# An LSTM step on one core: gate products of 512 columns cut into 256, and a verdict given by the sequencer

## What is computed

```python
def step(carry, x_t):
    h, c = carry
    sel_in = jnp.concatenate([h, c, x_t], axis=-1)
    logits = sel_in @ W_sel.T + b_sel
    onehot = jax.nn.one_hot(jnp.argmax(logits, axis=-1), Sx, dtype=x_t.dtype)
    g_all = jnp.einsum('bi,sgi->bsg', x_t, W_ih) + jnp.einsum('bh,sgh->bsg', h, W_hh) + b_ih + b_hh
    g = jnp.einsum('bsg,bs->bg', g_all, onehot)
    h2, c2 = _lstm_activate(g, c)        # sigmoid(f)*c + sigmoid(i)*tanh(g); sigmoid(o)*tanh(c)
    return ((h2, c2), h2)
```

## Time and profile before

| | |
|---|---|
| runs | 7712.02 us median of 3 (7709.5 to 7713.49) |
| the profiled execution | 7713.46 us, span 7711.7 us |
| PE busy | 6634.8 us (86%), 85,214 matmuls |
| PEld busy | 3513.4 us (46%) |
| DVE busy | 3545.5 us (46%) |
| ACT, POOL busy | 1004.7 us (13%), 945.3 us (12%) |
| granted TensorE clock, mean | 0.963 |

### The profile page before, as it was taken

One profiled execution on the slowest core, in us unless ns is written; L12 is line 12 of the kernel. 1 busy time (PEld: TensorE's weight loads), 2 busy tenths in 40 slices (PEclk: granted clock), 3 DMA queues, 4 the chain that ended last, 5 costly groups with the idle time before them and its releaser, 6 DMA issues. The chain is left out here.

```text
span 7711.7 us, 250693 instructions
## 1 busy us (share of the span) xinstructions
PE 6634.8 (86%) x85214; PEld 3513.4 (46%) x85215; DVE 3545.5 (46%) x16895; ACT 1004.7 (13%) x4031; POOL 945.3 (12%) x2829
## 2 busy tenths in 40 slices
PE   3467998899999998888888888888888888888888
PEld 3433444655555554444444444444444444444444
DVE  5523112355555554444444444444444444444444
ACT  0011001311111111111111111111111111111111
POOL 5703112200000000000000000000000000000000
PEclk6588998999999999999999999999999999999999
DMA  3220001622222210000000000000000000000000
GB/s 83 0 68 0 0 0 40 224 78 81 80 84 77 83 56 8 4 8 4 8 8 4 8 4 8 6 7 8 4 8 7 6 8 4 8 4 8 8 4 24
DMA packets 292938, 220.00 MB, mean 29 GB/s; under 512 B 137196, under 2 KB 268652, under 8 KB 290609
## 3 DMA queue, kind: packets, MB, share of 16 engines
q1 hardware_dynamic: 162612, 160.58, 6.2%
q10 hardware_dynamic: 106110, 59.01, 3.0%
q0 software_dynamic: 24192, 0.10, 1.0%
HBM read 160.28 MB, written 59.36 MB: 28 GB/s over the span
## 5 line engine op out<-in xcount | busy, mean ns | idle before, releaser
L1021 PE MATMUL ps<-WH,hparts 128*17 128x512 f16 x49760 | 2969.1, 380 | 148.9 <-DVE hparts L864 63.7
L1021 PEld LDWEIGHTS ps<-WH,hparts 128*17 128x17 f16 x49760 | 1305.0, 91 | 1316.2 <-DVE hparts L864 242.7
L840 DVE STREAM_TRANSPOSE gateT<-ps 128x512 f32<-128x512 f32 x1250 | 896.0, 717 | 2097.2 <-PE ps L1057 2088.0
L1091 PE MATMUL ps<-WH 128*128 128x512 f16 x4970 | 1246.1, 381 | 0.0
L467 POOL COPY xT<-hfull 128x4 f32 x1250 | 239.9, 192 | 5386.9 <-DVE hparts L862 5386.9
L1008 PE MATMUL ps<-wselT,acts 128*1 128x4 f32 x10000 | 430.5, 166 | 407.1 <-DVE acts L852 407.1
L972 PE MATMUL ps<-O,Adj 128*128 128x512 f16 x3000 | 650.3, 380 | 77.2 <-DVEq L749 77.2
L1091 PEld LDWEIGHTS ps<-WH 128*128 128x128 f16 x4970 | 404.6, 97 | 630.8 <-issue 278.7
L581 ACT ACTIVATE gateT<-gblk 128x16 f32 x1250 | 289.3, 231 | 2660.9 <-DVE pick L835 2618.4
L585 ACT ACTIVATE acts<-gates 128x16 f32<-128x16 f32 x1250 | 269.8, 216 | 2239.8 <-DVE gates L844 2239.8
L1065 PE MATMUL ps<-xT,wih_next 128*128 x2048 | 501.1, 388 | 65.1 <-DMA wih_next<-in_w_ih 34.0
(11 more groups left out here) (141 smaller groups left out, 4547.4 us busy)
## 6 DMA issues: line engine op xcount, KB each, us to landing
wih_next<-in_w_ih SPq DMA_DIRECT2D x256, 256.0 KB, 2.9
gblk<-gate_inputs ACTq DMA_DIRECT2D x48, 800.0 KB, 5.0
gate_inputs<-gx_next SPq DMA_DIRECT2D x64, 500.0 KB, 2.6
wst<-in_w_hh ACTq DMA_DIRECT2D x32, 512.0 KB, 7.6
wih<-in_w_ih SPq DMA_DIRECT2D x16, 1024.0 KB, 8.6
adjacency<-Adj SPq DMA_DIRECT2D x2, 6400.5 KB, 24.7
Adj<-adjacency SPq DMA_DIRECT2D x2, 6400.0 KB, 26.8
gate_inputs<-gstage SPq DMA_DIRECT2D x16, 500.0 KB, 6.0
```

What stands on the lines that cost most here:

```text
L840: dve.transpose(gateT[:, :, 0:32], gate_ps.rearrange("p (c q) -> p c q", q=32)).then_inc(turned, 1)
L1021: nc.tensor.matmul(gate_ps[32 * j:32 * j + 17, :], hparts[:, k, :], WH[:, s * KC + k, part, j, :], start=(k == 0 and part == 0), stop=(k = ...
L1091: nc.tensor.matmul(ps[:, 2, :], WH[:, 0, 0, 0, 0:P], WH[:, 0, 0, 0, :], start=True, stop=True)
```

## The change

The 32 matmuls of 512 columns become 64 of 256 columns, over the same weights. `hparts` gets two columns more; the first 4 matmuls of each eight read it from column 1 and take the first two gates, the other 4 read it from column 0 and take the other two gates, so that these land one row lower (rows 1 and 17 beside 0 and 16) in the same 256 columns of PSUM. The transpose reads 256 columns in place of 512. The seal is gone: the last four products count `guess_mm`, and DVE also waits for `settled`, which either the sequencer counts, where guess and verdict agree, or the last four of the repeated products. The branches on the guess stand ahead of the logits, so that each of the four copies now holds logits, products and verdict; the guess for the next step is read behind the products. On DVE, c comes before `osig`, and `owsel` is made from `acts` directly; all logits wait for `owsel_ready`.

```diff
-        gateT = sb("gateT", [P, G * SUB, 33], f32)
+        gateT = sb("gateT", [P, 2 * SUB, 48], f32)
...
-        hparts = sb("hparts", [P, SUB, 17], f16)
+        hparts = sb("hparts", [P, SUB, 19], f16)
...
-                dve.wait_ge(gates_mm, n)
+                dve.wait_ge(guess_mm, n4)
+                dve.wait_ge(settled, n4)
                 dve.transpose(gateT[:, :, 0:32], gate_ps.rearrange("p (c q) -> p c q", q=32)).then_inc(turned, 1)
...
-                pe.wait_ge(c_ready, n)
+                pe.wait_ge(owsel_ready, n)
                 for k in range(SUB):
                     nc.tensor.matmul(logit_ps, acts[:, G * SUB + k:G * SUB + k + 1], wselT[:, k, :], start=False, stop=False)
-                pe.wait_ge(owsel_ready, n)
                 pe.wait_ge(tanc_ready, n)
...
+            def cell_products(s, done):
+
                 for k in range(KC):
                     for part in range(2):
                         for j in range(4):
-                            nc.tensor.matmul(gate_ps[32 * j:32 * j + 17, :], hparts[:, k, :], WH[:, s * KC + k, part, j, :],
-                                             start=(k == 0 and part == 0), stop=(k == KC - 1 and part == 1),
-                                             tile_position=(0, 32 * j))
...
+                            nc.tensor.matmul(gate_ps[32 * j:32 * j + 18, :], hparts[:, k, 1:19], WH[:, s * KC + k, part, j, 0:2 * P],
+                                             start=(k == 0 and part == 0), stop=False, tile_position=(0, 32 * j))
+                        for j in range(4):
+                            last = nc.tensor.matmul(gate_ps[32 * j:32 * j + 18, :], hparts[:, k, 0:18],
+                                                    WH[:, s * KC + k, part, j, 2 * P:4 * P],
+                                                    start=False, stop=(k == KC - 1 and part == 1), tile_position=(0, 32 * j))
+                            if k == KC - 1 and part == 1:
+                                last.then_inc(done, 1)
...
             def step(t, n):
-                pe.reg_load(guess, pick_row[0:1, bass.ds(t, 1)])
-                logits(t, n)
-                products_of(guess, n, True)
-                pe.wait_ge(pick_ready, n)
-                pe.sem_inc(pick_seen, 1)
-                pe.reg_load(chosen, pick[0:1, 0:1])
+                pe.reg_mov(guess, guess_next)
+
+                def guessed(s):
+                    logits(n)
+                    pe.wait_ge(h_ready, n)
+                    cell_products(s, guess_mm)
+                    pe.reg_load(guess_next, pick_row[0:1, bass.ds(t + 1, 1)])
+                    pe.wait_ge(pick_ready, n)
+                    pe.sem_inc(pick_seen, 1)
+                    pe.reg_load(chosen, pick[0:1, 0:1])
+                    with pe.If_eq(chosen, S - s):
+                        pe.sem_inc(settled, 4)
+
+                def repeated(s):
+                    cell_products(s, settled)
+
+                of_set(guess, guessed)
                 with pe.If_ne(chosen, guess):
-                    products_of(chosen, n, False)
-
-                nc.tensor.matmul(seal_ps, hparts[:, 0, 0:1], hparts[:, 0, 0:1], start=True, stop=True).then_inc(gates_mm, 1)
+                    of_set(chosen, repeated)
```

59 lines of the change are left out of this document (30 added, 29 removed).

## The result

The changed kernel takes 8414.08 us (median of 3 runs, 8409.18 to 8428.64) where the one before takes 7712.02: a ratio of 1.092, with a 95% interval of 1.089 to 1.094. The forecast was 8130, with a range of 7800 to 8430; the direction and most steps of the working are right, the sum is 284 us short, and the time is 16 us inside the upper end of the range. The profiled execution took 8428.64 us, 715 more than that of before, and its span is 8426.9 us.

The account below looks back on a forecast made before the run. It took the LSTM steps, 6200 of 7712 us, as a closed chain from h through products and transpose to h. Terms of -34, +173, +221 and +59 made +419 us, so 8130, with a range of 7800 to 8430.

Parts of the forecast that it names:

- early hits: Steps among the first 256 with a right guess: 181, each 4.79 to 6.01 us, 1.22 more, +221 us.
- late hits: Steps after the first 256 with a right guess: 763, each 4.48 to 4.43 us, together -34 us.
- late misses: Steps after the first 256 repeating products after a wrong guess: 231, each 0.75 us more to 6.95, +173 us.
- early misses: Steps among the first 256 repeating products after a wrong guess: 74, each 0.80 us more, together +59 us.
- The Trainium skill's 64 for TensorE: Rival on PE's instruction queue: 32 pairs of load and matmul wait, last pair passed at 0.8 us; 7840 us, 12%.
- PE's hand-over of the logits: Behind the verdict: first logits matmul at 3.9 us, last at 4.3, next products at 4.43 after the first product.
- Transpose to h: DVE's time from transpose to h: 2.34 - 0.27 = 2.07 us, the transpose itself falling from 0.72 to 0.45.
- the term for the verdict: Sequencer's work behind the 64th pair, from register instruction to count: 1.13 us, so `settled` is there at 2.13.
- The case of 17 pairs: Rival: 17 pairs of load and matmul wait, last passed at 1.24 us; +290 us, 8420 in all, 8%.
- The freed sequencer: Rival: PE's sequencer is not held by the queue, `settled` comes at 1.4 to 1.6 us; 7600 us, 15%.
- the slow weight loads: Rival: weight loads set the pace of 256-column groups, at 0.13 us a group 0.35 more a round; 8600 us, 5%.
- the likeliest case: Last of 64 pairs passed at 1.0 us, when 24 are left; 8130 us, own range 8030 to 8250, 60%.

## Why the prediction came out as it did

**Right.** The last of 64 pairs is passed with 24 left, and the run with 48 pairs shows that it is a count of pairs. Groups are 0.109 us apart, the transpose takes 0.450, `L1060` loads at 1.17 where I had 1.1, the compare is at 2.06 (2.0), PE idles 0.95 us in a late miss (1.0). From transpose to transpose, which I named as the check, early hits last 5.98 us (6.0), late hits 4.61 (4.43) and late misses 7.24 (6.95). That the early hits agree is luck: by the transposes the early misses last 8.67, where the forecast had 7.3, and both together lie 0.35 us a step above it. Nor does anything point to instructions loaded inside the steps: the page has 20 packets on the queue for them, where it had 15. The Trainium skill's 64 for TensorE (Advanced Engine Details and Errata, Engine Queue Depths; "complicated with tiling"), by which the time would have been 7840, is not what these tiled products show: 24 pairs are 48 instructions.

**Too small, by term.** Against the terms of the forecast's sum the late hits add 130 us, the late misses 67, the early hits 47 and the early misses 42. A late hit was to last 4.43 us by PE's hand-over of the logits, and that came at 4.45, by two errors that cancel: the last logits matmul starts at 4.44 and not at 4.3, and the products can follow it by 0.01 and not by 0.1. But DVE's chain, forecast at 4.26 + 0.05 and so hidden, came at 4.61 and decides. It is longer by three terms:
- *Transpose to h,* 2.187 us where I had 2.07. In the step "2.34 - 0.27 = 2.07" the transpose gained just its 0.27; but 0.07 went to the order of DVE's waits, which can be read in the order rows (`gx_set,turned` before, `turned,gx_set` now) and which I didn't price, 0.02 to the reduction over the wider layout (0.233 for 0.212), 0.03 to the register instruction. The run with the waits turned back shows the 0.07.
- *Count to transpose,* "settled is there at 2.13, the transpose starts at 2.19": 2.18 and 2.34. Some 0.07 of the 0.16 is again the place of the wait, by the same run (2.21 and 2.295 there); the rest I take for a sequencer's count on its way to DVE, for which the kernel before had no row.
- *The register instruction and the load behind the 64th pair,* 0.05 later than forecast, as is all that follows.

A late miss lacks 0.29 us: 0.08 at the start of the repeated round (2.88 for 2.8), 0.12 from its products to the transpose, which are the four counts (forecast, at 20 us in all, and left out of the sum) and the place of the wait, and 0.09 from there to the next products. An early miss lacks 0.24 by its length and 0.57 by its increase (1.37 for 0.80): its repeated round starts at 3.01 (2.8) and its unit at 5.16 (4.9), and before the change that unit started at 3.59 and not at the "about 4.0" that the forecast took off.

**Early hits** were forecast with 6.01 by products, and the trace has 6.40. 141 of them have 6.16. In the other 40 the unit behind the products takes 2.4 us from its first matmul's start to its last's, where the others take 1.58, and these steps last 7.26. The timeline of one that is not slow and of the next, which is:

```profile
1656.81 1.95 PE L1080 MATMUL ps<-xT,wih_next 128*128 x8 [1.89 <-DMA wih_next<-in_w_ih]
...
1662.94 3.10 PE L1080 MATMUL ps<-xT,wih_next 128*128 x8 [1.89 <-DMA wih_next<-in_w_ih]
```

and the windows around them, whose last three numbers are the granted clock, DMA's share and GB/s:

```profile
1650.00:1662.00 12.00, 8.48 (x180) 7.02 (x180) 5.62 (x26) 1.30 (x6) 0.73 (x4) 1.00 0.57 155
1662.90:1669.00 6.10, 5.65 (x90) 4.32 (x90) 2.00 (x10) 0.44 (x2) 0.36 (x2) 0.72 0.15 42
```

The unit of 3.10 us runs at a granted clock that is down to 0.72 in this stretch, the lower of the two levels for most of it (from the fourth on its matmuls start 0.42 us apart, in the others 0.21), after PE had stood idle for 1.89 us, as it does in the early hits now (1.79 in the mean of the 141, 1.93 in the 40). The forecast read a granted clock of 1.00 and had no term for that. The row names the DMA of the unit's weights as what ended the idle time; but in these hits it had landed 0.78 us before the unit's start in the median, so that it was the hand-over that held the unit. 40 x 1.09 = 44 us. The step behind such a unit is slower too: the 24 of the 141 that follow one last 6.47, the others 6.09. The clock is then some 56 us in all, and the 0.08 that are left of an early hit come from the unit, at 3.76 in those others where I had 3.6. In the kernels with the next guess loaded first, and with the verdict after 48 pairs, where the unit starts at 3.3 and 3.6 us after the first product in place of 3.86, no unit in the steps is slow; with the next guess loaded last and with DVE's waits the other way, where it starts at 3.82 and 3.84, 35 and 32 are. That the idle time brings the clock down was seen in these traces and not tested by itself.

**What the sum hid.** The load of the next guess was 0.31 + 0.06 in the term for the verdict. It was priced rightly, but ahead of the logits it costs far less: moving it there saves 392 us, more than half of the 702. And the forecast puts all of the loss on the 64 pairs. The runs with one half of the change show 225 us for the columns, 250 for the control flow and DVE's new counts and waits (142 of these in misses), and 227 that only arise together. Some 56 of the 227 are the clock, of which neither half loses any in these steps but for the unit of one early hit; for the rest the reading is that the pairs push the load and the branches behind PE's work, which fits the rows of both traces but was not tested by itself.

**The rivals.** The case of 17 pairs (8420) has the measured time, but not its mechanism: the queue passed 24 pairs. The freed sequencer falls with the rows of `L1060`, the slow weight loads with the 0.109 us between groups. So the range holds the time by luck: its upper end stands for a case that did not occur. Had it been built from the likeliest case alone (8030 to 8250), it would have missed; the terms left out were nearly all of one sign, waits and hand-overs between engines that the kernel before did not have, and the clock.

## What to carry to other kernels

Count how many instructions an engine's queue takes, in the trace, before doubling their number for the same work: whatever decides something (a load, a compare, a count that another engine waits for) must be handed over while the queue has room, so place it among the instructions, not behind them. What a register load on the sequencer costs depends on what stands behind it: the same load, moved to two other places, saved 392 us and 71. And where an instruction waits for two semaphores, write them so that the one that comes last is the one that stays on the instruction (here the first in the text; the trace shows which).

## What was not expected of the hardware

Which of two waits stands first in the text is worth 0.07 us per step. Four counts from side-by-side tiles reach the waiting engine 0.07 us later than one. PE fell to the lower level of its clock in the unit of 40 of 181 early hits, with 1.8 us of idle time ahead of each unit in the mean, and in 35 and 32 in the two other kernels with as much; in the kernels in which it was 1.6 us or less in the mean it did so in one hit alone, the second step of the kernel with 256 columns alone, where PE had stood idle for 5.8 us.
